# Third scores moved directly behind the transposed scores, and layer-norm statistics moved one expert ahead, in a feed-forward, attention, feed-forward kernel

## The reference, cut to what matters

```
x = x + 0.5 * ffn(layernorm(x))
x = x + attention(layernorm(x))      # 16 heads of 8 features, causal softmax
x = x + 0.5 * ffn(layernorm(x))
ffn:       shared swiglu + sum of the top 2 of 8 experts, each weighted by its softmax score
           swiglu(x) = (silu(x @ w1) * (x @ w3)) @ w2
attention: scores = Q K^T / sqrt(8), softmax over keys not after the query, times V, times W_O
```

## Time and profile before

| | |
|---|---|
| Three runs, us | 1253.01, 1240.52, 1249.53 (median 1249.53) |
| Profiled execution | 1246.44 us, span 1244.0 us, mean granted PE clock 0.968 |
| Busy, share of the span | PE 90%, PEld 55%, DVE 80%, ACT 64%, POOL 45% |
| First and last mask of the attention stage on POOL | start at 382.8 and 907.4 us |

### The profile page before, as it was taken

The page is one execution under the profiler, slowest core; times in us unless marked ns, Lnnn a source line. Parts: engine busy times, 40 slices in busy tenths (PEclk is TensorE's granted clock), DMA queues, the critical chain, the costliest instruction groups (busy, mean ns, idle before and its releaser), DMA issues. The chain is left out here.

```text
span 1244.0 us, 31981 instructions
## 1 busy us (share of the span) xinstructions
PE 1118.1 (90%) x11588; PEld 684.1 (55%) x11588; DVE 999.4 (80%) x2589; ACT 793.5 (64%) x1545; POOL 562.8 (45%) x722
## 2 busy tenths in 40 slices
PE   2899999999978999999999989999969999999998
PEld 1566665665624555555555555555536666665665
DVE  5788888888866888888887888888767888888886
ACT  4566666666625667676766766666745666666664
POOL 2566656656602333333333332333425666566565
PEclk9899999999967999999998999999979999999999
DMA  4442433423200000000000000000013443424332
GB/s 134 137 154 79 154 112 121 138 70 137 70 1 1 1 2 2 2 2 2 2 2 2 2 2 2 2 2 2 2 50 117 127 131 101 148 91 149 113 119 94
DMA packets 59865, 80.11 MB, mean 64 GB/s; under 512 B 5568, under 2 KB 26944, under 8 KB 59712
## 3 DMA queue, kind: packets, MB, share of 16 engines
q1 hardware_dynamic: 59712, 78.08, 19.7%
HBM read 73.34 MB, written 4.72 MB: 63 GB/s over the span
## 5 line engine op out<-in xcount | busy, mean ns | idle before, releaser
L696 POOL TENSOR_TENSOR h_lo<-h,h_hi 128x512 f16<-128x512 f32 x288 | 332.2, 1158 | 267.7 <-ACT h_hi L643 265.0
L1256 POOL TENSOR_SCALAR_AFFINE_SELECT probs_at<-probs_at 128x512 f32<-128x512 f32 x256 | 156.3, 634 | 349.0 <-ACT probs_at L1214 349.0
L1136 DVE TENSOR_REDUCE neg_max_at<-score_at 128x2 f16<-128x512 f32 (+1 forms) x384 | 254.4, 692 | 74.2 <-PE score_at L966 68.2
L1214 ACT ACTIVATE probs_at<-prob_at 128x512 f32<-128x512 f32 x384 | 201.7, 599 | 79.1 <-PE prob_at L998 77.2
L435 DVE TENSOR_TENSOR prod<-a,gate_wide 128x512 f32<-128x512 f32 x256 | 175.3, 685 | 84.3 <-ACT a L635 83.6
L563 PE MATMUL y_b<-w_hi,h_hi 128*128 128x128 f16 x1152 | 208.2, 219 | 30.2 <-POOL h_lo L696 30.2
L643 ACT ACTIVATE h_hi<-h 128x512 f16<-128x512 f32 x288 | 179.9, 625 | 64.6 <-DVE h L445 58.6
L563 PE MATMUL y_b<-w_lo,h_hi 128*128 128x128 f16 x1152 | 208.2, 219 | 0.0
L563 PE MATMUL y_b<-w_hi,h_lo 128*128 128x128 f16 x1152 | 208.2, 219 | 0.0
L635 ACT ACTIVATE a<-a 128x512 f32<-128x512 f32 x256 | 148.5, 580 | 61.4 <-PE a L547 60.4
L445 DVE TENSOR_TENSOR h<-prod,b 128x512 f32<-128x512 f32 x256 | 174.5, 681 | 5.6 <-issue 0.7
(11 more groups left out here) (139 smaller groups left out, 1966.7 us busy)
## 6 DMA issues: line engine op xcount, KB each, us to landing
gate_wide<-gate_rows SPq DMA_DIRECT2D x256, 256.0 KB, 5.1
x<-in_L_attn_x_dram SPq DMA_DIRECT2D x16, 256.0 KB, 6.0
out_dram<-x SPq DMA_DIRECT2D x16, 256.0 KB, 6.8
raw_w<-in_L_ffn_w_dram SPq DMA_DIRECT2D x3, 512.0 KB, 4.8
gate_rows<-gate_rows SPq DMA_DIRECT2D x32, 16.0 KB, 1.4
raw_w<-in_L_ffn_sw_dram SPq DMA_DIRECT2D x3, 64.0 KB, 3.6
raw_attn<-in_L_attn_W_Q_dram SPq DMA_DIRECT2D x1, 64.0 KB, 4.6
raw_attn<-in_L_attn_W_K_dram SPq DMA_DIRECT2D x1, 64.0 KB, 3.5
```

The source lines that it names most:

```text
L696: nc.gpsimd.tensor_tensor(h_lo[k][:, :], h[k][:, :], h_hi[k][:, :], ALU.subtract).then_inc(hlo_done, 1)
L1136: nc.vector.tensor_reduce(dst, src, AX.X, ALU.max, negate=True).then_inc(max_done, 1)
L1214: nc.scalar.activation(probs[j % 2][:, i, :], prob_bank[i][:, :], ACT.Exp, scale=SCALE).then_inc(exp_done, 1)
L1256: nc.gpsimd.affine_select(out=p, in_=p, compare_op=ALU.is_ge, fill=0.0, base=0, pattern=[[0, GROUPS], [1, P]], channel_multiplier=-1).then ...
```

## The change

In the feed-forward stages `residual` moves from step 4 to step 2 on DVE, the two halves of `stats` from steps 5 and 6 to 4 and 5, the moments from step 7 to 6, and POOL's `root` from behind the low part of step 7 to behind that of step 6. In attention, PE does `weigh` and part 3 directly behind `both`, and then all three places of jobs; part 3 is written by a new function, `last_scores`, in which the two heads come first (the first of them opens the bank) and the mask is added last. DVE takes the maxima of all three parts together, ahead of all jobs. ACT's and POOL's order in attention stays.

```
-                    if e == 4 and c > 0:
+                    if e == 2 and c > 0:
                         residual(c - 1)
-                    if e in (5, 6) and has_norm(c + 3):
-                        stats(c + 3, range(2 * e - 10, 2 * e - 8))
-                    if e == 7 and has_norm(c + 3):
+                    if e in (4, 5) and has_norm(c + 3):
+                        stats(c + 3, range(2 * e - 8, 2 * e - 6))
+                    if e == 6 and has_norm(c + 3):
                         norm_moments(dve, nc, norm0 + c + 3, buf, ln_step)
...
-                    if e == 7 and has_norm(c + 3):
+                    if e == 6 and has_norm(c + 3):
                         root(c + 3)
...
+            def last_scores(c, slot, b, j):
+
+                wait_count(pe, max_done, c * 24 + b * 12 + 3 * j + 1)
+                view = score_bank[(3 * j + 2) % 2][:, :].rearrange("p (h k) -> p h k", k=SEQ)
+                rows, first = unit_rows(j), b * SEQ
+                for h in range(2):
+                    nc.tensor.matmul(view[:, h, :], q_pack[slot][rows, 2 + h, first + P:first + SEQ],
+                                     k_pack[slot][rows, 2 + h, first:first + SEQ], start=(h == 0), stop=False,
+                                     skip_group_check=True)
+                nc.tensor.matmul(view[:, :, P:SEQ], consts["ident_b"][:, :],
+                                 consts["causal"][:, :].unsqueeze(1).to_broadcast([P, 2, P]),
+                                 start=False, stop=True, skip_group_check=True).then_inc(scored, 1)
...
-                        turn_jobs(job, c, slot, places[0])
                         if j > 0:
                             weigh(c, slot, b, j - 1)
...
                         if ahead:
-                            scores(*ahead, parts=(2,))
+                            last_scores(*ahead)
+                        turn_jobs(job, c, slot, places[0])
                         turn_jobs(job, c, slot, places[1])
                         turn_jobs(job, c, slot, places[2])
...
                         if ahead:
-                            maxima(ahead[0], *ahead[2:], parts=(0, 1))
+                            maxima(ahead[0], *ahead[2:])
                         turn_jobs(job, c, slot, places[0])
-                        if ahead:
-                            maxima(ahead[0], *ahead[2:], parts=(2,))
                         turn_jobs(job, c, slot, places[1])
```

## The result

The changed kernel takes 1283.34 us (median of four runs, 1279.87 to 1287.95) against 1245.41 us: a ratio of 1.031, 95% interval 1.026 to 1.035. It is slower, by more than the 1.8% that I named, inside the range of 1245 to 1298.

The account below looks back on a forecast made before the run. PE is busiest, but when a bank is given back was taken to matter too. 1246.4 - 32 (feed-forward) + 52 (attention) + 3 (clock) = 1269 profiled; the median 3.1 above, 1272 us, 1.8% slower; range 1245 to 1298.

Parts of the forecast that it names:

- The feed-forward term: Feed-forward: PE's stall behind POOL's low part of expert 8 goes whole, 28 x 1.15 = 32 us less.
- Root, ACT and cover: Feed-forward: root ends at 148.12, ACT scales from 148.15; covers of 0.6 us (step 7) and 1.0 us (expert 8).
- The attention order: Attention: new order of jobs, part 3 and maxima costs 3.40 us a turn, 52 us more in all.
- the ends: Attention's first and last turns: the last has nothing ahead from unit 3 on; sum 16 x 1.05 + 15 x 2.35.
- The unit's third job: Attention, two job banks: the third job waits until the first is taken; +0.36 to +0.72 us in units 1 to 7.
- The change of shape from `weigh` to the heads: PE in attention: 32-column to 32-row matmuls taken as one change, 0.10 us, with 0 to 0.2 as ends.
- The clock: Attention: PE idles in more places, so one more stretch at 1.2 GHz, 3 us added.
- The first rival: Attention: clock falls in every turn, up to 16 x 2.5 = 40 us, 1285 to 1312; chance 0.12.
- The other side: Attention: the new order pays because PE's stream counts, -40 us, 1178 with feed-forward's 32; chance 0.09.
- rival 2: Attention order pays if DVE and ACT take first jobs within about 0.6 us: -40, total 1178; chance 0.09.
- Rival 3: Feed-forward: the stall stays, moments or step 7's low part late; no gain there, 1304 us; chance 0.05.
- Rival 4: Both stages: attention +30 and feed-forward -32 cancel, 1248 us; chance 0.14 shared with half of rival 2's waits.

Follow-up runs that it names:

- e1: Only the feed-forward edits, attention as in the kernel before: 1212.21 us, ratio 0.973.
- e6: e1 with `residual` left in step 4 instead of moved to step 2: one run of 1218.59 us.
- e3: The changed kernel with place 0's jobs back ahead of `weigh` on PE alone, DVE's new order kept: 1324.78 us, ratio 1.061.
- e9: e2 with K01 taken by DVE instead of ACT: 1208.17 us, ratio 0.966.
- e7: The changed kernel with extra identity transposes filling all of PE's larger waits in attention: 1258.36 us, ratio 1.007.
- e2: The changed kernel with place 0's jobs back in their old place on PE and DVE, leaving feed-forward edits and mask last: 1205.50 us, ratio 0.967.
- e5: The changed kernel with twelve extra identity transposes on PE in unit 1, between `weigh` and part 3: 1297.12 us, ratio 1.034.

## Why the prediction was right, and where its size was off

The forecast was 1272 us and the median is 1283.34. In the profiled executions the change costs 34.2 us where the sum had 23, in three terms: feed-forward -33.5 for -32, the attention order 47 for 52, the clock 21 for 3. The first two errors made the kernel faster than forecast by about 6 us and hid part of the third, of 18.

*The feed-forward term* was 32 us less; it is 33.5 (18.5 and 15.0) by the profile, and e1 alone is 32.0 us below the kernel before in the medians (1212.21 and 1244.23). Root, ACT and cover came as worked out: the low part of step 7 starts at 142.41 right behind the shift, that of expert 8 is 1.3 us early (forecast 1.0), and no new wait appeared on PE. `residual` cost nothing (e6).

*The attention order* was 3.40 us a turn, 52 in all. The one turn without a fall shows 3.20. The stage shows 47: 567 us without the clock's part against e1's 520.5, which is all but free of falls. The rest of the miss is at the ends, where turn 0 is 2.0 us longer and the last one 0.1, for 3.4 and 1.05 in the sum. Seven of eight units are within 0.11 of the forecast, unit 6 within 0.14. The unit's third job behind the taking of its first is the mechanism: e3 moves the wait from one set of units to another just as that rule says, and e9 meets it in a place of its own.

*The change of shape from `weigh` to the heads*, which the trace of before did not hold, is one change and not two: in e7's unit 4 and in the changed kernel the heads follow `weigh` after 0.79, as the mask did (561.28 to 562.07; 558.01 to 558.80 in the earlier trace rows). One change costs 0.10 us. The Trainium skill (TensorEngine Tiling (Array Packing), Key Properties) says that a change of mode drains the array and gives no price; the 0.10 us agrees with some cost at each change. e2 shows that saving one is worth it only in the four units where PE leads.

*The clock* is the step that failed. The prediction put it as "I add one such stretch, 3 us"; it is 25 us. Before, the stage itself had 4 (2.8 for the 6.8 us fall, 1.25 for one of 3.4), so the change's share is 21. Everything else sums to 47 - 33.5 = 13.5, so that without the clock the kernel would be 1.1% slower, and with it is 3%. (The long falls around the stages' ends, 37.5 us from 348.5 before, 10.2 from 335.1 and 20.5 from 348.7 after, stand outside these sums.) What failed is that I took the falls before (twice in 16 turns) as a rate that would stay about the same, although each turn was to hold over 3 us more of idle PE: its printed busy share over the stage went from 91% to 82% (451.57 of 554). The first rival had the frequency right, and its price wrong: one fall in unit 1 costs 1.0 us and not 2.5. From the rows I read that PE doesn't lead all through it, as DVE's maxima of part 3 and its taking of o10 stand in that stretch; no run tests that alone. The rule of the Trainium skill that I set beside that rival (TensorE: Matmul & The Clock Gate, A second HAM failure mode: psum-queue depth-cycling) says that small idles between groups make the clock oscillate. With a fall in 13 of the 14 steady turns the changed kernel's trace agrees; e2's, where PE also has idle times between groups in the same banks (93 distances of over 0.5 us between starts) and no fall comes between 386 and 860 us, shows that such idles alone are not enough.

*The other side*, rival 2, needed DVE and ACT to take the first job in time. They don't: PE waits 1.03 us for m10 alone. Rival 3 is excluded by e1. Rival 4 had the halves cancel; they do not, by 13.5 us before the clock.

## What to carry to other kernels

With two rotating banks, the writer waits unless the time between its first and next use of a bank is longer than the taker's queue plus its work; moving work from between the jobs to ahead of them removes that distance although no instruction is added. Before such a move, list for each job who takes it and what stands ahead of it in that engine's list, and replay one period: here this gave the period to 0.6%. And give an idle term a second price, the clock: where the trace of before already shows a fall now and then, more idle time can make the falls regular. Last, test the parts of a reordering one by one: here one part (the mask last) was worth 0.36 us a turn, and was hidden under a part that cost ten times as much.

## What the runs showed of the hardware

Filling PE's waits with useless transposes is worth 25 us (1283.34 to 1258.36). Filling only the longest of them gains nothing (1297.12; its ratio of 1.034 is not to be told from the changed kernel's 1.031): the falls then come elsewhere, and longer. In e5 the clock stayed at 2.4 GHz through unit 1 and fell to 1.2 GHz in units 3 to 5 of 8 turns, where the changed kernel, with the same waits there, had kept it in 13 of 14. The Trainium skill (TensorE: Matmul & The Clock Gate, Part 4: PE-mode transpose) says that transposes don't count as busy in the same way; in e7 float32 transposes against an identity were all that was added, and the clock held. The trace prints them as MATMUL and doesn't show whether the mode that the page means is on; for transposes written this way the measurement decides, and they hold the clock.

A fall costs less than half its length: 1.0 us for 3.4 us in unit 1 of the changed kernel, 13.3 us for 37.5 us in e3, 2.8 us for 6.8 us in the kernel before, between 0.3 and 0.4 of the stretch. Executions of one kernel differ by it: the kernel before took 1240.46 us at a mean granted clock of 0.977 and 1258.83 us at 0.955. e1 and e6, with the same attention, hold 5.0 and 31.8 us of such time between their first and last mask, and those distances differ by 9.7 us. What picks the moment of a fall is open.
